# Mix stages of an eight-stage fp32 transformer kernel: eight batches as one unrolled stream of units, three score slots, masked keys by GpSimd a batch ahead

## What is computed

```python
def _L1_ffn_ref(x, Wq, Wk, Wv, Wo, Wff):      # HEADS = 16, dh = 8, D = 128
    q, k, v = split_heads(x @ Wq), split_heads(x @ Wk), split_heads(x @ Wv)
    scores = jnp.einsum('bqd,bkd->bkq', q, k) / jnp.sqrt(jnp.asarray(D, x.dtype))
    attn = jax.nn.softmax(scores, axis=-1)
    out = jnp.einsum('bkq,bkv->bqv', attn, v)
    z = out.reshape(B, H, S, dh).transpose(0, 2, 1, 3).reshape(B, S, L)
    z = _l2_normalize(z @ Wo)
    z = _l2_normalize(z @ Wff)
    return jax.nn.gelu(z, approximate=False)
```

## Time and profile before

| what | value |
|---|---|
| median of three runs (lowest, highest) | 6548.77 us (6543.41, 6562.14) |
| the profiled execution, its own time | 6545.28 us |
| span of the profiled execution | 6543.5 us |
| mean granted TensorE clock, share of full | 0.845 |
| first mix call, first projection to first tail matmul | 5658.41 to 5919.85 us |
| second mix call, the same | 6254.19 to 6512.2 us |

### The profile page before, as it was taken

How to read it: one execution, slowest core, us unless ns; L and a number is a source line. 1 busy time by engine, 2 the same in 40 slices (tenths; PEclk the granted TensorE clock), 3 DMA queues, 4 the chain that set the end, 5 groups by cost and what they waited for, 6 DMA issues and landing times. The chain is left out here.

```text
span 6543.5 us, 177007 instructions
## 1 busy us (share of the span) xinstructions
PE 5082.6 (78%) x69200; PEld 3250.3 (50%) x69200; DVE 3856.2 (59%) x6192; ACT 4305.5 (66%) x8847; POOL 2494.6 (38%) x963
## 2 busy tenths in 40 slices
PE   1000069999999999977777899999999998687688
PEld 0000046666666666633333566666666666343443
DVE  4555556666666666655555566666666665546844
ACT  4333347777777777749999677777777776456655
POOL 0000045555555555514444555555555654000000
PEclk6555589999999999976666899999999999667866
DMA  1000022222222222200000222222222221000000
GB/s 48 0 0 0 0 66 55 67 58 60 60 61 64 57 63 60 52 12 1 0 0 1 57 65 59 62 59 64 57 64 60 61 60 41 9 0 3 0 2 7
DMA packets 181302, 248.00 MB, mean 38 GB/s; under 512 B 52076, under 2 KB 80232, under 8 KB 180072
## 3 DMA queue, kind: packets, MB, share of 16 engines
q1 hardware_dynamic: 176264, 221.95, 13.7%
q10 hardware_dynamic: 4320, 15.73, 0.8%
HBM read 43.50 MB, written 5.24 MB: 7 GB/s over the span
## 5 line engine op out<-in xcount | busy, mean ns | idle before, releaser
L401 PE MATMUL PS<-arena 128*128 128x512 f32 x2304 | 1171.0, 604 | 25.8 <-ACT arena L763 17.3
L1070 POOL TENSOR_TENSOR arena<-arena 128x1024 f32<-128x1024 f32 x192 | 551.8, 2874 | 932.7 <-DVE arena L969 932.7
L1070 POOL TENSOR_TENSOR lns<-arena 128x1024 f32<-128x1024 f32 x192 | 543.1, 2828 | 653.5 <-DVE arena L969 640.2
L939 DVE TENSOR_REDUCE arena<-PS 128x16 f32<-128x1024 f32 x192 | 235.1, 1225 | 773.3 <-PE PS L428 773.3
L958 DVE TENSOR_REDUCE arena<-arena 128x32 f32<-128x2048 f32 x192 | 438.9, 2286 | 395.5 <-ACT arena L763 395.5
L1440 PE MATMUL PS<-arena 128*128 128x512 f32 x8 | 5.6, 862 | 803.4 <-DVE arena L1374 803.4
L765 ACT ACTIVATE arena<-PS 128x512 f32<-128x512 f32 x384 | 229.9, 599 | 561.6 <-PE PS L401 558.2
L1073 POOL TENSOR_TENSOR lnc<-arena 128x1024 f32<-128x1024 f32 x192 | 546.5, 2846 | 0.0
L455 PEld LDWEIGHTS PS<-arena 64*64 64x64 f32 x24576 | 472.7, 134 | 145.1 <-issue 137.4
L1073 POOL TENSOR_TENSOR arena<-arena 128x1024 f32<-128x1024 f32 x192 | 541.1, 2818 | 0.0
L762 ACT ACTIVATE arena<-PS 128x512 f32<-128x512 f32 x768 | 481.4, 627 | 66.1 <-PE PS L401 42.8
(11 more groups left out here) (263 smaller groups left out, 11468.3 us busy)
## 6 DMA issues: line engine op xcount, KB each, us to landing
arena<-arena SPq DMA_DIRECT2D x2880, 64.0 KB, 2.0
arena<-in_L_ffn_Wqkv ACTq DMA_DIRECT2D x30, 512.0 KB, 4.1
arena<-in_L_ffn_Wo SPq DMA_DIRECT2D x48, 128.0 KB, 2.8
scratch<-arena SPq DMA_DIRECT2D x4, 1024.0 KB, 4.7
arena<-scratch SPq DMA_DIRECT2D x4, 1024.0 KB, 7.8
arena<-in_L_ffn_W SPq DMA_DIRECT2D x12, 341.0 KB, 3.0
arena<-in_L_ffn_Wqkv SPq DMA_DIRECT2D x6, 512.0 KB, 4.8
arena<-in_ffn_scales SPq DMA_DIRECT2D x12, 128.0 KB, 3.2
```

The lines of the kernel that those rows point to most:

```text
L401: pe.matmul(PS[:, QKV + bank, :], xs[uu % 2][:, par * P:(par + 1) * P], w, start=True, stop=True).then_inc(qkv_ready, 1)
L1070: pool.tensor_tensor(halves(heads(t2)), halves(heads(raws[par]))[:, :, ::-1, :], sine, ALU.mult)\
```

## The change

The 64 units of a stage become one stream, written out without a hardware loop. Four things are different.

1. There are three score slots (`RING = 3`, banks 0 to 5), three buffers for exponentials and for statistics, and two for query, masked keys and values. Scores(u) wait for the exponentials of u-3, and the exponentials of u for heads(u-3).
2. TensorE's loop is as before, scores(u+2) and heads(u), but runs over batch boundaries. VectorE now does shift(0), shift(1), and then for each unit shift(u+2) and values(u).
3. The projection reads the normalised input itself (no copy) and comes in two pieces through bank 7: query and key at unit 2, values at unit 4 of the batch before. The key's masks are made by GpSimd (L1828), the query is scaled when it is copied.
4. The maximum is negated by the reduction itself (`negate=True`), so the scaling instruction goes.

```diff
+        RING = 3
+        mx_e = [hd.take(4 * T).rearrange("p (h t q) -> p h t q", h=2, t=2) for _ in range(RING)]
+        mx_st = [hd.take(16) for _ in range(RING)]
+        mx_q = [hd.take(T) for _ in range(2)]
+        mx_m = [[hd.take(T) for _ in range(HEADS_IN_GROUP)] for _ in range(2)]
+        mx_v = [hd.take(2 * C).rearrange("p (t n) -> p t n", t=2) for _ in range(2)]
...
         def mix_tensor(pe, run, call, n0):
...
+            first = (run * B + 1) * PAIRS8
...
+            def project(b):
+                g = run * B + 1 + b
+                pe.wait_ge(hd_projected, g * 3)
+                x = XN[:, b * T:(b + 1) * T]
+                for k in range(2):
+                    last = pe.matmul(PS[:, MIX_PROJ, k * T:(k + 1) * T], hd_w[k], x, start=True, stop=True)
+                last.then_inc(hd_proj, 1)
...
+            def scores(u):
+                b, n = divmod(u, PAIRS8)
+                g = run * B + 1 + b
+                if n == 0:
+                    pe.wait_ge(hd_masked, (g + 1) * HEADS_IN_GROUP)
+                    pe.wait_ge(hd_projected, g * 3 + 2)
+                if u >= RING:
+                    pe.wait_ge(hd_exp, first + u - RING + 1)
...
+            def heads(u):
+                b, n = divmod(u, PAIRS8)
+                if n == 0:
+                    pe.wait_ge(hd_copied, run * B + 1 + b)
+                pe.wait_ge(hd_v_ready, first + u + 1)
...
+            project(0)
+            project_values(0)
+            scores(0)
+            scores(1)
+            for u in range(UNITS_MIX):
+                b, n = divmod(u, PAIRS8)
+                if n == 2 and b + 1 < B:
+                    project(b + 1)
+                if n == 4 and b + 1 < B:
+                    project_values(b + 1)
+                if u + 2 < UNITS_MIX:
+                    scores(u + 2)
+                heads(u)
...
         def mix_scalar(act, run, call, n0):
...
+            def copy_keys(b):
+                g = run * B + 1 + b
                 act.wait_ge(hd_proj, g * 2 + 1)
                 act.wait_ge(hd_masked, g * HEADS_IN_GROUP)
+                act.activation(hd_k, PS[:, MIX_PROJ, T:2 * T], ACT.Copy).then_inc(hd_projected, 1)
+                act.wait_ge(hd_scores, (g - 1) * PAIRS8)
+                act.activation(mx_q[b % 2], PS[:, MIX_PROJ, 0:T], ACT.Identity, scale=MIX_SCALE).then_inc(hd_projected, 1)
...
+            for u in range(UNITS_MIX):
+                b, n = divmod(u, PAIRS8)
+                exps(u)
+                if n == 0 and b > 0:
+                    copy_out(b - 1)
+                if n == 3 and b + 1 < B:
+                    copy_keys(b + 1)
+                if n == 5 and b + 1 < B:
+                    copy_values(b + 1)
+            copy_out(B - 1)
...
         def mix_vector(dve, run, call, n0):
...
+            def shift(u):
+                dve.wait_ge(hd_scores, first + u + 1)
+                dve.tensor_reduce(mx_st[u % RING][:, 0:4], PS[:, 2 * (u % RING):2 * (u % RING) + 2, :]
+                                  .rearrange("p h (t q) -> p (h t) q", t=2), AX_X, ALU.max, negate=True).then_inc(hd_bias, 1)
+
+            def values(u):
...
+                dve.wait_ge(hd_exp, first + u + 1)
+                dve.reciprocal(st[:, 8:12], st[:, 4:8]).then_inc(hd_recip, 1)
...
+                dve.tensor_tensor(to, fr, rc, ALU.mult).then_inc(hd_v_ready, 1)
+            shift(0)
+            shift(1)
+            for u in range(UNITS_MIX):
+                if u + 2 < UNITS_MIX:
+                    shift(u + 2)
+                values(u)
...
+        def mix_gpsimd(pool, run):
...
+            for b in range(B):
+                g = run * B + 1 + b
+                pool.wait_ge(hd_projected, g * 3 + 1)
+                pool.wait_ge(hd_scores, (g - 1) * PAIRS8)
+                for v in range(HEADS_IN_GROUP):
+                    only = hd_only[:, v:v + 1].broadcast_to([P, T])
+                    pool.tensor_tensor(mx_m[b % 2][v], hd_k, only, ALU.mult).then_inc(hd_masked, 1)
```

More of the change, by code:

```diff
@@ L1620, in mix_sync, with score_banks @@
             sp.dma_start(hd_only, d["c_only"]).then_inc(hd_loaded, 16)
[L1623 to L1630, removed]
+        UNITS_MIX = B * PAIRS8
+        MIX_OUT, MIX_PROJ = 6, 7
+        def score_banks(u):
+            return PS[:, 2 * (u % RING):2 * (u % RING) + 2, :].rearrange("p h (t q) -> p h t q", t=2)
         def mix_tensor(pe, run, call, n0):
@@ L1634, in mix_tensor @@
             wait_alone(pe, hd_loaded, 16 * 6 * (run + 1))
[L1635 to L1668, removed]
@@ new lines, in heads @@
+            def heads(u):
[3 more added lines that the diff above has]
+                pe.wait_ge(hd_v_ready, first + u + 1)
+                for t in range(2):
+                    for s in range(2):
+                        grp, v = head_of(n, s)
+                        at = grp * VGROUP + v * GROUP
+                        last = pe.matmul(PS[grp * GROUP:(grp + 1) * GROUP, MIX_OUT, 0:T], hd_vm[:, t, at:at + GROUP],
+                                         mx_e[u % RING][:, s, t, :], start=(v == 0 and t == 0),
+                                         stop=(v == HEADS_IN_GROUP - 1 and t == 1), skip_group_check=True)
+                last.then_inc(hd_out, 1)
@@ L1722, in mix_scalar, with copy_out, exps @@
-            project_scalar(act, run * B + 1, 0)
-            copy_projected(run * B + 1)
-            with act.Fori(0, B - 1) as b:
-                batch(run * B + b + 1, b, False)
-            batch(run * B + B, B - 1, True)
+            def copy_out(b):
+                act.wait_ge(hd_out, first + (b + 1) * PAIRS8)
+                act.activation(hd_Z[:, b * T:(b + 1) * T], PS[:, MIX_OUT, 0:T], ACT.Copy).then_inc(hd_copied, 1)
+            def exps(u):
+                st = mx_st[u % RING]
+                act.wait_ge(hd_bias, first + u + 1)
+                if u >= RING:
+                    act.wait_ge(hd_out, first + u - RING + 1)
+                for s in range(2):
+                    for t in range(2):
+                        k = 2 * s + t
+                        last = act.activation(mx_e[u % RING][:, s, t, :], score_banks(u)[:, s, t, :], ACT.Exp,
+                                              bias=st[:, k:k + 1], scale=1.0, accum_out=st[:, 4 + k:5 + k])
+                last.then_inc(hd_exp, 1)
@@ L2503, in _ @@
                     b0_gpsimd(pool)
+                if part == "mix":
+                    mix_gpsimd(pool, run)
                 meet(pool, K + 1)
```

109 lines of the change are left out of this document (36 added, 73 removed).

## The result

| what | before | after |
|---|---|---|
| median (lowest to highest, runs) | 6553.88 us (6543.41 to 6562.14, 4) | 6780.9 us (6776.34 to 6788.53, 4) |
| the profiled execution, its span | 6545.28, 6543.5 us | 6788.53, 6786.7 us |
| mean granted clock | 0.845 | 0.827 |
| first call, first projection to first tail matmul | 261.4 us | 373.9 us |
| second call, the same | 258.0 us | 378.6 us |

The ratio is 1.0348 [1.0328, 1.0369]: 3.5% slower. The two profiled spans differ by 243.2 us, and the two stages hold 236.2 of it (114.5 and 121.7); the other stages differ by 7 in all.

The account below looks back on a forecast made before the run. No engine bounds the whole kernel; the mix stages wait for TensorE. A call sums 12.7 + 347.7 + 6.2 + 19.6 = 386.2, +124.8, less 23.1 plus 2: +103.7; two calls, +207, give 6,756 us, range 6,680 to 6,812.

Parts of the forecast that it names:

- The ring: Mix-stage units: scores, reduction, multiply and values follow one another without overlap; 5.70 us against 3.86, or 3.84 at high clock.
- The credit for high clock: Mix stages: one 6.8 us high-clock stretch kept behind each of seven projections, saving 3.3 each, 23.1 us a call.
- the seven projections: On TensorE, in two pieces ahead of scores, seven times a call: 2.8 us each at low clock, 19.6 together.
- the start: From a call's first projection to its first value group: 12.7 us, including 1.7 for exposed GpSimd masks.
- the end: At a call's end, two value groups without scores between, and the way to the tail: 6.2 us.
- The masks: On GpSimd, four a batch, 2.9 to 11.5 us: hidden except in the first batch, 2.9 instead of 1.14, +1.7.
- Copies: On ScalarE, input copy removed and query scaled in its copy: 1.8 a unit plus some 0.2, hidden, so nothing.
- third slot: Score buffers: it loosens the scores' wait on exponentials, not the last wait in mid-batch, so it does not help.
- What would show it: Mid-batch signs: reduction 2.1 us after scores, TensorE idle 1.7 before L1681, clock near 0.55, stages 360 us each.
- The clock holds: Rival, 8%: mix stages keep the full clock between projections; nearly all periods at 3.84, 262.7 a call, 6,551 us.
- The ring does not close: Rival, 4%: the multiply does not wait for the reduction ahead; 6,342 us at high clock, some 6,590 at low.
- The clock and the Trainium skill: Mid-batch: gapless quarter-tile work stayed at 0.50 for 23.9 us, while the skill says continuous work brings the full clock.

Follow-up runs that it names:

- one filler: The changed kernel with one extra full-array matmul behind each unit's scores, except at a batch's first unit; 6697.28 us, ratio 1.0224.
- two ahead: The kernel before with VectorE's reduction two units ahead of the multiply and statistics in three buffers; 6743.32 us, ratio 1.0292.
- two fillers: The changed kernel with two extra full-array matmuls behind each unit's scores, except at a batch's first unit; 6586.2 us, ratio 1.0043.
- one ahead: The changed kernel with VectorE's reduction one unit ahead of the multiply instead of two; 6344.12 us, ratio 0.9675 to the kernel before.
- masks on VectorE: The kernel one ahead, with a batch's four masks made by VectorE behind the fifth unit's multiply instead of GpSimd; median 6380.44 us, ratio 0.9718.
- pairs: The kernel one ahead, with TensorE taking units two by two, four exponential buffers and reductions three ahead of the values; 6319.07 us, ratio 0.9633.

## Why the prediction was right, and where it was not

*The ring.* Right, with one piece a little too long. Scores to reduction 2.13 (predicted 2.12), reduction to reciprocal 1.14 (1.26), reciprocal and multiply 0.46 (0.40), signal 0.06 (0.06), values to scores 1.85 (1.86): 5.64 against 5.70. The 1.26 was the distance to the scaling, which had to wait for the reduction's own result; the reciprocal of an older unit does not, and started before the reduction's recorded end. The whole unit came out 0.06 shorter, 3.7 us a call over 61 periods. At high clock 3.84 was predicted and 3.83 measured, in the kernel with one filler.

*The credit for high clock.* This term was mis-sized: "I keep one stretch of 6.8 us behind each of the seven projections", 23.1 us a call. Behind the start, the trace of after has six stretches of 3.4 us in the first call and two in the second. With the measured unit a call all at low clock would be 12.7 + 344.0 + 6.2 + 19.6 = 382.5; it took 373.9 and 378.6, so high clock gave back 8.6 and 3.9. (Adding up the shortened units of the first call gives 8.2. The remainder comes so close by luck, since the other terms were off and cancel: the start took 10.5 instead of 12.7, the end 4.1 instead of 6.2, the seven projections 2.00 and 1.15 each, 22.1 instead of 19.6, and the boundaries another 1.5.) The step that failed is carrying the 6.8 us over from the projection of before. The ring by itself doesn't end them: in the kernel before with two ahead, where the projection still comes in one piece with two groups of values and two of scores behind it, they are there in six of the seven batches; in after a stretch lasts half as long. Each kernel, one stretch:

```profile
5754.80:5761.60 6.80, 3.71 (x39) 2.23 (x37) 3.94 (x9) 3.71 (x15) 0.00 (x0) 1.00 0.00 0
...
5735.70:5739.10 3.40, 1.69 (x16) 0.69 (x12) 1.50 (x3) 1.38 (x7) 2.16 (x4) 1.00 0.00 0
```

Whether the split of the projection or the groups that no longer come together is the reason, no run separates. The forecasts for the two stretches, 363.1 and 359.7 (the 261.4 and 258.0 of before plus 101.7), were 10.8 and 18.9 short: the credit makes 14.5 and 19.2 of that, the unit takes 3.7 off each, and the 3.4 us that the second call was to keep did not come. For the profiled execution the sum was 6,752 and 6,788.5 came: 29.7 of this miss lies in the stretches, 7 in stages that the change leaves alone. Against the median it is 25 (6,756, 6,781), inside the range of 6,680 to 6,812.

*The masks.* 613 ns each (L1828), below the lower bound of 0.72 that was scaled from the 128x1024 multiply. TensorE waited for them only at the start of a call, 1.1 us ahead of the first scores. That made the start shorter than the sum had it; nothing else hung on it.

*Copies, third slot.* The copies are hidden, as said: ScalarE's busy time is 134.2 a call (136.41 before) and its exponentials wait for VectorE alone. "The third slot does not help" fits the trace, in which TensorE's matmuls never stand idle for exponentials in the first call, but no run took the slot out of the closed ring; with the ring open it is worth 14 us.

*What would show it.* Reduction 2.13 after the scores, 1.71 idle before L1681 with L1799 as releaser, ScalarE's wait moved to the bias: all there. The clock was 0.53 and 0.51 (0.55), and the stages 374 and 379 (360), from the same credit.

*The rivals.* "The clock holds" did not happen. Its price, 6,551, is borne out in size by the two fillers: 6586.2 with a granted clock of 0.92. (The "near 6,650" for half the units doesn't fit the prediction's own terms: 30 periods at 1.86 us less each, taken from all low, give some 6,690.) "The ring does not close" did not happen either, but its terms are those of one ahead: 158 a call predicted, 156.4 measured; 6,342 us predicted, 6344.12 measured; 2.0 a unit predicted, by ScalarE, 2.05 measured, by TensorE. So the change with the reduction one ahead is good for 3.25%, and the order of one reduction takes it all and 3.5% more.

*The clock and the Trainium skill.* Mid-batch before, gapless work was at 0.50; the masks on VectorE show the same for 160 us at 98% busy. The Trainium skill (TensorE: Matmul & The Clock Gate, section "Why this matters for your kernels") has continuous work bring the full clock; these rows disagree, and the measurement decides. With its other half, that a clock once won stands short gaps, one ahead agrees (157 us at 1.00 with TensorE busy 150.33), the ring does not (its six high stretches in the first call lasted 3.4 us each, with idle times of 1.7 us in every unit).

**What stays open** is what makes the clock rise within a call. With the masks on VectorE it took 160 us in the first call and 24 in the second of one execution; in one ahead 17.1 us, in which TensorE stood idle for 4, and that in both calls of both profiled executions. No run here isolates the cause.

## What to carry to other kernels

Looking further ahead on one engine is only free if what it looks at was issued, on the other engine, before work that doesn't depend on the looking. Follow the in-order programs of both engines around once and ask where the ring closes: here reduction(u+2), in front of multiply(u), waits for scores issued directly before values(u), and at high clock a ring of 3.83 us takes the place of a unit of 2.05. A stall of this kind may cost twice, once as idle time and once as the clock of the work between; and a deep change should be timed with each of its orders apart, since a good 3% can hide behind one line.

## What the runs showed of the hardware

- One program can spend long times at either level of the granted clock: with the masks on VectorE the trace has 160.4 us at 0.50 with TensorE busy 157.44 of it, then 81.9 us at 1.00 with 73.65 busy. Four executions took 6351, 6352, 6409 and 6413 us.
- More work made the kernel faster: two 128x128x256 matmuls behind each group of scores, 216 records a call, took 195 us off (6780.9 to 6586.2), by raising the clock from about 0.52 to 0.92.
- A GpSimd multiply of 128x256 took 613 ns where one of 128x1024 took 2,874: less than a quarter, 719.
- Two units of scores issued behind each other (16 records) took 1.63 us at full clock in the pairs, and 1.16 to 1.17 at the start of a batch before, where a unit of 8 among values took 1.06.
- The value matmuls of two units, which fill four column groups of 32, took 1.01 us at full clock when both were ready, where one unit's took 0.99.
